# Value products of four tiles moved from the tile loop into the triangular solve

## The reference

```python
def step(carry, inp):
    s, mem = carry
    qt, kt, vt, sdt, abt, bbt = inp
    ...
    s = s * alpha[..., None]
    u = jnp.einsum('bhd,bhdv->bhv', kt, s)
    s = s - beta[..., None] * jnp.einsum('bhd,bhv->bhdv', kt, u)
    s = s + beta[..., None] * jnp.einsum('bhd,bhv->bhdv', kt, vt)
    out = jnp.einsum('bhdv,bhd->bhv', s, qt)
    return ((s, mem), out)
```

## Time and profile before

| | us |
|---|---|
| three runs, median | 1876.25 |
| lowest and highest of them | 1864.84, 1890.15 |
| the profiled execution | 1873.82 |
| its span, first to last instruction | 1871.8 |
| TensorE busy in it | 1449.1 |
| VectorE busy | 1274.1 |
| ScalarE busy | 634.8 |
| GpSimd busy | 360.1 |

### The profile page before, as it was taken

One profiled execution on the slowest core, in us unless ns is written; L12 is line 12 of the kernel. 1 busy time (PEld: TensorE's weight loads), 2 busy tenths in 40 slices (PEclk: granted clock), 3 DMA queues, 4 the chain that ended last, 5 costly groups with the idle time before them and its releaser, 6 DMA issues. The chain is left out here.

```text
span 1871.8 us, 46841 instructions
## 1 busy us (share of the span) xinstructions
PE 1449.1 (77%) x18540; PEld 946.9 (51%) x18568; DVE 1274.1 (68%) x3341; ACT 634.8 (34%) x1342; POOL 360.1 (19%) x515
## 2 busy tenths in 40 slices
PE   1687988797878887787879786888869897974685
PEld 0343664365525653465436562566436663652665
DVE  5568576966787667866796578765695678534564
ACT  4430243223422262134312352124312442222564
POOL 1210141014201320015101420023001420110232
PEclk8568996899689987998789979896699968996898
DMA  8980001010010001000100001000101000102223
GB/s 252 322 254 18 8 8 30 2 23 20 8 23 21 5 20 29 18 8 19 30 13 12 20 8 23 21 5 19 30 11 19 13 14 12 24 26 99 69 70 125
DMA packets 128139, 81.97 MB, mean 44 GB/s; under 512 B 75185, under 2 KB 118513, under 8 KB 127922
## 3 DMA queue, kind: packets, MB, share of 16 engines
q1 hardware_dynamic: 124466, 69.94, 13.6%
q0 software_dynamic: 3456, 8.95, 1.5%
HBM read 27.72 MB, written 51.15 MB: 42 GB/s over the span
## 5 line engine op out<-in xcount | busy, mean ns | idle before, releaser
L789 POOL COPY kx<-kend_t 32x256 f32<-32x256 f32 x256 | 114.3, 447 | 807.3 <-PE ps L1349 787.5
L1286 PE MATMUL ps<-wv,ident 128*128 128x512 f32 x320 | 173.7, 676 | 10.6 <-DVEq L1654 10.5
L1729 DVE SCALAR_TENSOR_TENSOR state<-state,gam,ps 128x128 f32<-128x128 f32 x512 | 137.4, 339 | 49.1 <-PE ps L1349 49.1
L1673 DVE TENSOR_TENSOR nv<-ps,nrm 128x512 f32<-128x512 f32 x64 | 44.2, 691 | 175.9 <-PE ps L1209 175.4
L1349 PE MATMUL ps<-w,kx 128*64 128x128 f32 x2048 | 127.1, 277 | 0.0
L1643 DVE TENSOR_TENSOR nv<-kq,kq_blk 128x31 f32<-128x31 f32 (+15 forms) x248 | 113.7, 458 | 16.7 <-ACT mem L852 10.8
L1349 PEld LDWEIGHTS ps<-w,kx 128*64 128x64 f32 x2048 | 111.7, 138 | 12.9 <-issue 12.9
L1521 DVE TENSOR_TENSOR kq_leaf<-kq,eleaf 128x1024 f32<-128x1024 f32 x32 | 39.9, 1247 | 112.6 <-ACT kq L882 112.4
L1286 PEld LDWEIGHTS ps<-wv,ident 128*128 128x128 f32 x320 | 66.7, 218 | 94.0 <-issue 77.5
L233 PE MATMUL ps<-eleaf,wf 128*128 128x512 f32 x112 | 62.0, 681 | 50.9 <-DVEq L1654 31.8
L999 ACT ACTIVATE w<-ps 128x512 f32<-128x512 f32 x64 | 38.2, 597 | 173.8 <-PE ps L1307 173.8
(11 more groups left out here) (313 smaller groups left out, 3303.9 us busy)
## 6 DMA issues: line engine op xcount, KB each, us to landing
slot_d<-row SPq DMA_DIRECT2D x16, 2064.0 KB, 20.3
xin<-slot_d SPq DMA_DIRECT2D x39, 129.0 KB, 2.1
a_d<-yt SPq DMA_DIRECT2D x8, 512.0 KB, 2.6
kq_blk<-a_d SPq DMA_DIRECT2D x32, 128.0 KB, 2.8
u_d<-kq SPq DMA_DIRECT2D x8, 512.0 KB, 2.6
ub<-u_d SPq DMA_DIRECT2D x128, 32.0 KB, 1.9
wall<-in_w SPq DMA_DIRECT2D x8, 512.0 KB, 7.9
xt<-in_xT POOLq DMA_DIRECT2D x8, 256.0 KB, 3.4
```

Of the source, the lines that this page charges most:

```text
L789: m = pool.tensor_copy(kx[part, :, b4, :], kend_t[part, g, 2 * q:2 * q + 2, :])
L1286: pe.matmul(bw.t[:, :], ident[:, :], wv[:, 0:512], start=True, stop=True)
L1729: k = dve.scalar_tensor_tensor(out=state[:, hp, b, :], in0=state[:, hp, b, :], scalar=gam[:, hp, b:b + 1], in1=bd[j].t[:, DV * x:DV * x + ...
```

## The change

The value products of tiles 0 to 3 are formed during the solve. TensorE issues the value matmul of tile 1 at pace 0, of tile 2 at pace 3 and of tile 3 at pace 5, each after the head's stage of that pace and ahead of the warm-up matmuls; each waits until the bank `bv` has been emptied of the tile before. ScalarE empties it: four ACTIVATE instructions a tile, one for each head, 128x128 from PSUM with the key norm as the scale of each partition. They write into `kq_leaf` and `kq_pair`, two tiles each, which nothing reads any more at that point of the chunk. In ScalarE's order tile 0 comes behind the head's gate, tile 1 behind the head's `rs`, tile 2 behind the second tanh, tile 3 behind the fourth. VectorE's `values` for tiles 0 to 3 and TensorE's for tiles 1 to 3 leave their former places; r(0) to r(3) read the new buffers. Tiles 4 to 7 stay as they were.

```diff
--- before.py
+++ after.py
@@ -518,6 +518,7 @@
     unit_rows = [t[:, 2 * j:2 * j + 2, :].rearrange("p h v -> p (h v)") for t in (nv, ysq) for j in range(2)]
     yss, yr = sb("yss", [P, H]), sb("yr", [P, H])
     kx = sb("kx", [P, 2, GB, P])
+    scaled_values = [t[:, j, :].rearrange("p (h v) -> p h v", v=DV) for t in (kq_leaf, kq_pair) for j in range(2)]
     attn = hd.attn
 
     psum = [ctx.enter_context(nc.psum_tensor(f"ps{i}", [P, 512], F32)) for i in range(8)]
@@ -939,6 +940,21 @@
                 act.wait_ge(kx_ready.sem, kx_ready.at(c, TILES, 1))
             act.activation(kend_t[:, :, p, :], b.t[:, :].rearrange("p (g k) -> p g k", g=NG),
                            ACT.Copy).then_inc(b.drained.sem, 1)
+
+        def values(c, i):
+
+            g, q = i // 2, i % 2
+            if i == 0:
+                act.wait_ge(norm_step.sem, norm_step.at(c, 3))
+                for name in ("leaf", "cross"):
+                    b = bank_of[f"{name}{HP - 1}"]
+                    act.wait_ge(b.full.sem, b.filled(c, f"{name}{HP - 1}"))
+            act.wait_ge(bv.full.sem, bv.filled(c, f"v{i}"))
+            for hq in range(4):
+                u = 8 * (2 * q + hq // 2) + 2 * g + hq % 2
+                m = act.activation(scaled_values[i][:, hq, :], bv.t[:, DV * hq:DV * hq + DV], ACT.Copy,
+                                   scale=nrm[:, 0, u:u + 1])
+            m.then_inc(bv.drained.sem, 1)
 
         def body(c, nxt, last):
             keys(c, 0)
@@ -976,10 +992,20 @@
                 drives(nxt)
             if last:
                 head_on_scalar(act, last, room, "gate")
+            values(c, 0)
+            if last:
                 load_exp_log_table(nc, act)
                 head_on_scalar(act, last, room, "rs")
-                for t in range(FT):
+            values(c, 1)
+            if last:
+                for t in range(2):
                     head_on_scalar(act, last, room, t)
+            values(c, 2)
+            if last:
+                for t in range(2, FT):
+                    head_on_scalar(act, last, room, t)
+            values(c, 3)
+            if last:
                 load_exp_log_table(nc, act)
                 for stage in ("rstd0", "xt", "rstd1"):
                     head_on_scalar(act, last, room, stage)
@@ -1282,6 +1308,8 @@
                 settle(c)
                 if last and n in stages:
                     head_on_tensor(pe, last, room, stages[n], lambda: settle(c))
+                if n in (0, 3, 5):
+                    values(c, (0, 3, 5).index(n) + 1)
                 for k in range(KEEP_WARM):
                     pe.matmul(bw.t[:, :], ident[:, :], wv[:, 0:512], start=True, stop=True)
             if nxt:
@@ -1289,7 +1317,7 @@
             for i in range(TILES + 1):
                 g, q = i // 2, i % 2
                 if i < TILES:
-                    if i + 1 < TILES:
+                    if 4 <= i + 1 < TILES:
                         values(c, i + 1)
                     if nxt and i + 1 < STEPS:
                         decays(nxt, i + 1)
@@ -1663,13 +1691,7 @@
 
             g, q = i // 2, i % 2
             dve.wait_ge(bv.full.sem, bv.filled(c, f"v{i}"))
-            if i == 0:
-                dve.wait_ge(tri_done.sem, tri_done.at(c, 1))
-
-            if i:
-                dve.wait_ge(bp.drained.sem, bp.emptied(c, f"p{i - 1}"))
-            elif later(c):
-                dve.wait_ge(bp.drained.sem, bp.emptied(c, f"p{TILES - 1}", 1))
+            dve.wait_ge(bp.drained.sem, bp.emptied(c, f"p{i - 1}"))
             dve.tensor_tensor(nv[:, :, :].rearrange("p (a h) v -> p a h v", h=2),
                               bv.t[:, :].rearrange("p (a h v) -> p a h v", h=2, v=DV),
                               quad(nrm[:, 0, :], g, q).unsqueeze(3).broadcast_to([P, 2, 2, DV]),
@@ -1701,7 +1723,6 @@
             if nxt:
                 silus(nxt)
             solve(c, nxt, last)
-            values(c, 0)
             if last:
                 head_on_vector(dve, last, room, "aff")
             if nxt:
@@ -1716,9 +1737,10 @@
                         dve.wait_ge(bw.full.sem, bw.filled(c, f"w{TILES - 1}", 1))
                     dve.wait_ge(bv.drained.sem, bv.emptied(c, f"v{i}"))
                     dve.wait_ge(bp.full.sem, bp.filled(c, f"p{i}"))
-                    dve.tensor_tensor(r[:, :, :], nv[:, :, :], bp.t[:, :].rearrange("p (h v) -> p h v", v=DV),
+                    scaled = scaled_values[i] if i < 4 else nv
+                    dve.tensor_tensor(r[:, :, :], scaled[:, :, :], bp.t[:, :].rearrange("p (h v) -> p h v", v=DV),
                                       ALU.subtract).then_inc(bp.drained.sem, 1)
-                    if i + 1 < TILES:
+                    if 4 <= i + 1 < TILES:
                         values(c, i + 1)
                 if i:
                     n = i - 1
```

## The result

The changed kernel took 1924.33 us (median of four runs, 1913.62 to 1935.8), the kernel before 1874.6 (four runs, 1864.84 to 1890.15). The ratio is 1.026, 95% interval 1.017 to 1.035: slower by 49.7 us, where a gain of 12 was forecast. (Medians in this document are over all runs of a kernel; a ratio with its interval compares fast runs alone, those at most 1.5% above the kernel's fastest, so it is not the quotient of two medians.) The profiled execution took 1935.8 us (span 1933.4, mean granted clock 0.827 against 0.860 before).

The account below looks back on a forecast made before the run. VectorE was taken to bound the solve and TensorE the tile loop. The terms -15.4 - 1.7 + 4.8 + 0.3 gave -12.0 us against the profiled 1873.82 us, forecast 1862, range 1845 to 1882.

Parts of the forecast that it names:

- The loop, tiles 2 and 3: Tile loop: each value matmul removed from TensorE gives back 0.96 us, 1.92 us per chunk, 15.4 us in eight chunks.
- the 2 us of cover: Tile loop: r(2) ends about two microseconds before TensorE would want it, so the whole 0.96 us counts; likewise for tile 3.
- The value matmul fills a wait. Worth at most 0.1 us: Loop start: tile 1's value matmul runs while TensorE's wad matmul awaits a bank from VectorE; removing it gains at most 0.1 us.
- (b): Rival: the solve's TensorE falls to the low clock behind its pace 0 wait; +6 us, so 1880; chance 0.11.
- (d): Rival: chunks with a late wad matmul at the solve's end change; three either way are 7 us, 1855 or 1869; inside forecast's 0.68.
- 0.8 us (0.5 to 1.2): Solve: scaling 0 on ScalarE delays the mean square, so VectorE newly waits before h2; chunks 1 to 6 lose 4.8 us.
- the 1.13 us that was assumed: Solve: ScalarE's four scalings take 1.13 us a tile, bounds 0.9 and 1.5; 4.5 us a chunk on ScalarE.
- for 0.3: Solve of chunk 7: the mean square starts late for another reason, so the loss was taken as 0.3 us.
- At pace 3 nothing was lost: Solve: tile 2's value matmul delays the next feed-forward pair, but stays under the cover at full clock; booked 0.
- The start of the loop: Between solve and r(0): removing VectorE's product of tile 0 gains about 0.1 us, since VectorE then waits for the wad matmul.
- The 1.7 us for chunk 0: Loop start of chunk 0, with no head stages: 0.61 us for VectorE's product and 1.05 for an earlier wad matmul, once.

Follow-up runs that it names:

- e2: Changed kernel plus one idle 512-column warm-up matmul where tile 1's value matmul stood at the loop's start: 1891.68 us, ratio 1.011 to the kernel before.
- e4: Changed kernel with an idle matmul at the loop's start and tile 1's value matmul moved behind the mean square: 1857.52 us, ratio 0.996 to the kernel before.
- e1: Kernel before with only tile 1's value matmul cut from 512 columns to 8: 1910.22 us, ratio 1.018 to the kernel before.
- e3: Changed kernel with tile 1's value matmul moved from pace 0 to pace 2, behind the head's mean square: 1890.47 us, ratio 1.011 to the kernel before.
- e8: e5 plus one idle warm-up matmul ahead of the first `w` matmul of tile 6: 1859.96 us, ratio 0.998 to the kernel before.
- e9: Kernel before plus idle warm-up matmuls in the three output turns and ahead of tile 6's first `w` matmul: 1862.88 us, ratio 1.001 to the kernel before.
- e6: Kernel before plus one idle warm-up matmul between the two transposes of each of three output turns: 1863.41 us, ratio 1.001 to the kernel before.
- e5: e4 plus one idle warm-up matmul between the two transposes of each of three output turns: 1858.77 us, ratio 0.998 to the kernel before.

## Why the prediction was wrong

The sum had -12.0 us and the runs +49.7, outside the range; every rival was too low as well. Step by step:

**The loop, tiles 2 and 3: right.** 0.96 us each was forecast, 0.95 measured between w(1) and w(2) and 0.86 (e2, e4) between w(0) and w(1). TensorE never waited for r(2) or r(3); the 2 us of cover held.

**"The value matmul fills a wait. Worth at most 0.1 us": the step that failed.** Read as time on the path it is true, since its place then is a pause. But the matmul was not free to take away. Without it the third wad pair and nearly all of tile 0 run at 1.2 GHz. In chunks 1 to 6 tile 0 takes 12.8 us where 8.76 - 0.96 = 7.8 was forecast, 5.0 us each; over the eight chunks 31.0 + 8 x 0.96 = 38.7 us. e1 shows that taking away the matmul's columns alone does this, e2 that one idle matmul undoes it. The prediction feared a low clock behind the pause at pace 0 (b) and weighed the end of the solve (d); it never asked what the removed matmul did for the clock. Removing work was costed as removing its duration.

**Tile 6 and tile 4: not in the sum.** w(6) to w(7) was 14.4 us in three chunks and 17.4 in two, instead of 11.6; with tile 4 this is 18.7 us. With e2 it is 12.8 and with e4 7.4, nearly all in tile 4 there; in the kernel before the same intervals were long in single chunks too (14.39 in chunk 5, 14.76 in chunk 4). That the slow tile 0 brings the later ones is not shown, as e1's chunks 3 and 6 had a good tile 0 and a slow tile 6. This part stays open.

**The solve, "0.8 us (0.5 to 1.2)": the mechanism was right, the size not.** ScalarE's four scalings took the 1.13 us that was assumed. The wait before h2 came where it was forecast, and was 2.0 to 2.1 us in chunks 1 to 5, 2.8 in chunk 6 and 2.2 in chunk 7 (for 0.3). In chunk 2 the value matmul takes 1.84 us to its hand-over instead of 0.9 and the warm-ups 4.00 instead of 3.54: together 1.4 us, because they run, wholly or in part, at the low clock behind the pause of 1.90. To this comes the wait of 1.1 us (1.5 in chunk 7) at the `ff` matmuls, for which nothing was booked. So the solves cost 23.2 us, 15.2 of them before h2 and 8.1 at the `ff` matmuls (by the waits); that is as much as rival (b) gave for them, and in part by its mechanism, the low clock behind the pause. (The Trainium skill, page "TensorE: Matmul & The Clock Gate", section "Why this matters for your kernels", warns of idle gaps between bursts of matmuls, but only of longer ones than this. Here the trace differs, and the measurement decides: behind the pause of 1.90 us the pair took 2.04 us instead of 1.02.) e3 shows that the order at pace 0 is the cause of the wait before h2: behind the mean square, the same scaling and the same matmul cost nothing there. The wait at the `ff` matmuls stays in four chunks of e3 and one of e4 and comes up in five of e8 and one of e9, so its cause is open. At pace 3 nothing was lost in chunk 2, as booked: the first feed-forward pair took 1.96 us behind 0.69 us of idle time.

**The start of the loop: right, and small.** 0.1 us was forecast for VectorE's product of tile 0; e4 shows 0. The 1.7 us for chunk 0 can't be told from chance: its stretch went from 9.11 to 6.98 us, but in e9, with the code of before there, it was 6.55. Rival (d) had three chunks either way at 7 us: in chunks 4 to 6 the late wad is gone (11.23 to 11.47 us before, 9.1 after), which is 6.9 us gained, and chunks 1 to 3 lose 2.6 (8.3 to 9.1). The late wad may be more than chance: all four kernels with the old order have two or three chunks of 11.2 to 12.1 us there (before, e1, e6, e9), and of the changed ones none has a chunk over 9.5. No run tests this.

**Open.** Which pause costs the clock varies between executions and chunks, for equal instructions. Where gains come back can be read, why cannot: from e9 to e8 the loops of the profiled executions lose 11.2 us, and the solves take back 6.9. The fronts hide much of the rest. No edit touches them, yet the profiled executions have them at 13.9 us less (e3) to 3.4 more (e2) than before's in the sum; in the kernel before alone the front of chunk 2 took 63.5 us at a mean granted clock of 0.73 and that of chunk 6 took 71.2 at 0.63. A gain of the size forecast is no larger than this.

## What to carry to other kernels

A matmul that fills a wait may be what keeps TensorE's clock up for the stage behind it: ahead of taking one away, look at the granted clock there, and price the next stage at the lower level as a rival. Put an idle matmul in the gap first: e2 told within one run that the clock was the loss, and in e6 and e9 such matmuls cost nothing that could be measured. A stretch that is mended is not yet time gained, as e5 to e8 show, so go by the total. Where work moves into another engine's shadow, put it behind the instructions that the critical engine waits for, not ahead of them.

## What the hardware showed that I had not expected

At the low level, a full TensorE did not bring the clock back soon. In chunk 2 of the kernel after, tile 0 kept the engine busy for 12.53 of 12.80 us with small matmuls, and the granted clock stayed at 0.5 from 590.3 until 603.9. The same instructions at clock 1.00 (7.58 us busy of 7.90 in e2) did not lose it. One 512-column matmul of 1.02 us ahead of them made the difference, 12.8 against 7.9 us.
